# Solving a 64-token chunk by its 32x32 diagonal inverses instead of a 64x64 inverse, and a new order of small products in a TensorE-filled loop

## The chip, the cores and the metric

The kernel runs on one core of a Trainium2 chip. The time is device microseconds of one execution; the kernel before was run three times. All work of the program lies in one launch, and nothing is computed outside it.

## What is computed

The reference is one transformer block over x of shape (4, 2048, 256): a delta-rule linear attention with 4 heads of 64, in chunks of 64 tokens, and a gated MLP of four layers, each behind a layernorm whose scale, shift and gate come from a conditioning vector. Cut to what the change touches, for each sequence, head and chunk:

```python
A0 = -where(strict, (wk @ wk.T) * L, 0)        # 64 x 64, strictly lower
A = inv(eye - A0)                              # unit lower triangular
def step(S, ...):                              # over the 32 chunks
    v_new = A @ v - (A @ wk) @ S               # = A @ (v - wk @ S)
    o = rk_g @ S + intra @ v_new
    S = gamma_C * S + wk_g.T @ v_new
```

After it come the output product with Wr, the gated residual (x1), a second layernorm, and the MLP: `silu(h w1) * (h w2)` of width 1024, then two 1024 x 1024 layers with gelu (l2 and l3 below), then 1024 to 256 (y).

## The kernel before

The kernel walks 32 steps (`STEPS`), one for each chunk of 64 tokens of all 4 sequences, 256 tokens in all. The recurrence over the state S forces the order of the attention parts; the MLP has no such order. So the program is a pipeline written out by hand: in step n the PE stream is the l3 layer and the last product y of chunk n-2, then l1 and l2 of chunk n-1, and between these long, dense products stand short *visits* of the attention of chunk n. The steps 3 to 30 run in a loop whose body holds 14 of them (`PASS`), the others are written out. Step 0 runs alone (list `alone`), step 1 in two pieces (`opening`, `second`).

What stands where is told by the table `between` (lines 278 to 297 of the profile's file): its key is an MLP item such as ("l2", 1), the second of the eight output blocks of layer l2, and its value lists the parts that come behind it. `walk` runs through that order for **each engine in turn**, and every engine carries out its own share of each part (`part` in each engine's block); semaphores tie them together, and each engine works strictly in that order. The normalisation of the next chunk hangs on the same items (`next_norm`).

The MLP products are 128x128 weights times 256 columns in a single-pass format (w_hi with act_hi and act_lo). The attention works in fp32, where the trace has two MATMUL records for one product; a record is called a **pass** below. Its products are small and go to pieces of the array: `half(c)` names 64 partitions, the 64 tokens of the chunk for two of the four sequences; `quarter(c, i)` names 32 of them, i the first or second half of the chunk. (e, q) run over these two sequences times four heads, m = e * 4 + q from 0 to 7. The visits of the attention in a step, by PE lines:

- start: h and r are turned (L1087, L1091) into `duo[0]`, behind l2's last block
- long visit behind ("l3", 1): gram (L1109, into `duo[1]`), pred (L1115, into `duo[0]`), values (L1101, into `solo[0]`), inter (L1124)
- ("ln2", 0) behind ("l3", 5): the normalised x1, `xn2`, is turned (L1207, into `solo[1]`)
- n 1 to n 3 behind l1's blocks 1, 4 and 7: the 32x32 diagonal inverses by a series (L1143; L1145 and L1152; L1147), each with 32 or 64 products of 32x32
- mi behind ("l2", 1), L1161: 16 products of 32x32, corner of the matrix times the lower inverse; ACT copies the result to `mi` (L656)
- upd behind ("l2", 2), L1170: 16 more of 32x32, times the upper inverse; meanwhile ACT spreads `inv_t` into the block-diagonal 64x64 `invT` (L661), then copies the corner in (L668)
- new behind ("l2", 4), L1181: 16 products of 64x64, `invT` times the corrected values v, into `solo[1]`; ACT copies them to `vn` (L673)
- state behind ("l2", 5) (L1189, L1191) and attn_out behind ("l2", 6) (L1198)

On the other engines the parts that matter are: ACT copies of gram (L647), v (L643), o_state (L650); POOL multiplies gram by masks (L535, `lv`) and decays the state (L578); DVE makes `intra` (L806), subtracts the prediction from v (L813, `u_ready`), runs the substitution fs 0 to fs 3 (L817 on) on the first masked gram, and makes `xn2` (L875, part norm2). MLP work on ACT is L705 and L706, on DVE L776.

At the start of step 2 PE runs eight products into `solo[1]` that nothing reads (L1080) and then waits until the last weight blocks have been rounded on ACT and POOL (`rounded`).

## Time and profile before

| | us |
|---|---|
| three runs | 1855.87, 1856.35, 1859.41 |
| median | 1856.35 |
| profiled execution, its time | 1858.39 |
| its span | 1856.6 |
| PE busy | 1807.0 (97%) |
| DVE, ACT, POOL busy | 1147.4, 989.2, 613.3 |
| mean granted TensorE clock | 0.987 |

Read it by the spacing of the MATMUL records on PE: their durations overlap, so the distance from start to start is what a product costs. The profile's page shows a clock of 7 tenths in the first two of its 40 slices and 9 tenths or more in all others.

### The profile page before, as it was taken

What the parts mean: (1) busy time and instruction counts of PE and PEld (TensorE: products, weight loads), DVE (VectorE), ACT (ScalarE), POOL (GpSimd) and SP (SyncE); (2) the same over time, 40 slices, a digit from 0 to 9 for tenths busy, and PEclk for the clock granted to TensorE, in tenths of its full rate; (3) what the DMA queues carried; (4) which work ended last, traced back from release to release, by engine and by line L of the source; (5) the groups of instructions that cost most, each with busy time, mean ns of one, the idle gap of its engine ahead of it and who ended that gap; (6) DMA issues with size and microseconds to landing.
All of it is one profiled execution on the core that took longest, in us unless ns stands there. A gap on an engine that the chain in (4) does not pass through costs nothing.

```text
span 1856.6 us, 66857 instructions
## 1 busy us (share of the span) xinstructions
PE 1807.0 (97%) x28606; PEld 1725.4 (93%) x28606; DVE 1147.4 (62%) x3044; ACT 989.2 (53%) x2318; POOL 613.3 (33%) x691
## 2 busy tenths in 40 slices
PE   4699999999999999999999999999999999999998
PEld 3599999999999999999999999999999999999998
DVE  5665666665666665666665666665666665666632
ACT  5564555554555554555555555555555555555454
POOL 3343233333233333233333233233233333233211
PEclk7799999999999999999999999999999999999999
DMA  8000000000000000000000000000000000000000
GB/s 322 20 14 20 8 20 19 20 14 20 8 20 19 20 14 20 8 19 19 19 14 19 8 19 19 19 14 20 8 19 20 19 14 20 8 19 20 15 2 13
DMA packets 33011, 44.04 MB, mean 24 GB/s; under 512 B 8324, under 2 KB 24840, under 8 KB 32712
## 3 DMA queue, kind: packets, MB, share of 16 engines
q1 hardware_dynamic: 30736, 37.19, 6.7%
q8 instruction: 230, 3.77, 0.8%
q10 hardware_dynamic: 1976, 2.51, 0.5%
q14 instruction: 69, 0.57, 0.1%
HBM read 22.78 MB, written 8.39 MB: 17 GB/s over the span
## 4 chain that ended last, share of the span: by engine, by line
PE 94%; issue 2%; DVE 2%; POOL 1%; ACT 1%; ACTq 0%; POOLq 0%; DVEq 0%
PE mlp L991 61%; PE mlp L1050 6%; PE solo L991 4%; PE solo L1101 3%; PE duo L1198 3%; PE solo L1181 2%; PE duo L1147 1%; PE duo L1143 1%; PE duo L1145 1%; PE duo L1189 1%; PE duo L1161 1%; PE duo L1170 1%; PE duo L1152 1%; PE duo L1124 1%; PE duo L1109 1%
## 5 line engine op out<-in xcount | busy, mean ns | idle before, releaser
L991 PE MATMUL mlp<-act_hi,w_hi 128*128 128x256 f32 x4096 | 1005.5, 288 | 0.4 <-POOL act_lo L569 0.2
L991 PE MATMUL mlp<-act_lo,w_hi 128*128 128x256 f32 x4096 | 973.0, 279 | 0.0
L991 PEld LDWEIGHTS mlp<-act_hi,w_hi 128*128 128x128 f32 x4096 | 770.4, 188 | 13.4 <-POOL act_lo L569 0.4
L991 PEld LDWEIGHTS mlp<-act_lo,w_hi 128*128 128x128 f32 x4096 | 769.4, 188 | 0.8
L705 ACT ACTIVATE full<-mlp,scale_sb 128x256 f32<-128x256 f32 x512 | 244.2, 477 | 558.6 <-PE mlp L991 557.1
L776 DVE TENSOR_TENSOR act_lo<-full,act_hi 128x256 fp32r<-128x256 f32 x512 | 243.1, 475 | 415.6 <-ACT act_hi L706 415.6
L569 POOL TENSOR_TENSOR act_lo<-full,act_hi 128x256 fp32r<-128x256 f32 x256 | 186.9, 736 | 505.3 <-ACT act_hi L695 505.2
L706 ACT ACTIVATE act_hi<-mlp,scale_sb 128x256 fp32r<-128x256 f32 x512 | 240.7, 470 | 0.0
L991 PE MATMUL mlp<-xh,w_hi 128*128 128x256 f32 x768 | 182.7, 279 | 5.4 <-ACT w_hi L627 5.4
L535 POOL TENSOR_TENSOR lv<-gram,level_mask 128x256 f32<-128x256 f32 x192 | 158.0, 849 | 84.1 <-DVE low L817 79.7
L991 PE MATMUL mlp<-xl,w_hi 128*128 128x256 f32 x768 | 182.3, 279 | 0.0
L515 POOL TENSOR_TENSOR rstd<-ve,minus_half 128x2 f32<-128x2 f32 x64 | 49.4, 772 | 398.2 <-DVE ve L743 398.2
L991 PEld LDWEIGHTS mlp<-xh,w_hi 128*128 128x128 f32 x768 | 145.4, 189 | 5.6 <-ACT w_hi L627 5.6
L690 ACT ACTIVATE gate<-mlp,scale_sb 128x256 f32<-128x256 f32 x192 | 91.2, 475 | 111.1 <-PE mlp L991 100.0
L889 DVE SCALAR_TENSOR_TENSOR full<-mlp,scale_sb,gate 128x256 f32<-128x256 f32 x192 | 92.7, 483 | 88.1 <-ACT gate L690 88.0
L991 PEld LDWEIGHTS mlp<-xl,w_hi 128*128 128x128 f32 x768 | 145.5, 190 | 0.0
L1050 PE MATMUL mlp<-w_hi,act_hi 128*128 128x256 f32 x512 | 124.3, 284 | 0.7 <-DVE act_lo L776 0.6
L1050 PE MATMUL mlp<-w_hi,act_lo 128*128 128x256 f32 x512 | 124.0, 281 | 0.0
L515 POOL TENSOR_TENSOR rinv<-ssm,minus_half 128x8 f32<-128x8 f32 x32 | 52.5, 1642 | 203.0 <-DVE ssm L766 203.0
L695 ACT CAST act_hi<-full 128x256 fp32r<-128x256 f32 x256 | 101.8, 398 | 8.3 <-DVE full L889 8.3
L1050 PEld LDWEIGHTS mlp<-w_hi,act_hi 128*128 128x128 f32 x512 | 96.5, 188 | 1.1 <-DVE act_lo L776 1.1
L1050 PEld LDWEIGHTS mlp<-w_hi,act_lo 128*128 128x128 f32 x512 | 96.4, 188 | 0.0
(161 smaller groups left out, 2591.1 us busy)
## 6 DMA issues: line engine op xcount, KB each, us to landing
w_raw<-in_wts SPq DMA_DIRECT2D x22, 512.0 KB, 10.0
xin<-in_x SPq DMA_DIRECT2D x64, 128.0 KB
out_y<-y SPq DMA_DIRECT2D x64, 128.0 KB, 2.5
kg<-r SPq DMA_DIRECT2D x64, 126.0 KB
wmod_sb<-in_wmod ACTq DMA_DIRECT2D x1, 1024.0 KB, 8.1
kg<-last SPq DMA_DIRECT2D x64, 2.0 KB
last<-r SPq DMA_DIRECT2D x64, 2.0 KB, 1.7
wmod_sb<-in_wmod ACTq DMA_DIRECT2D x1, 512.0 KB, 4.9
```

Source lines behind the costliest of these rows:

```text
L515: pool.tensor_tensor(dst[:], src[:], minus_half[:, 0:src.shape[1]], ALU.pow).then_inc(done, 1)
L535: return pool.tensor_tensor(lv[slot][:, e].rearrange("p (b q) n -> p b (q n)", b=NB), gram[:, e].rearrange("p (b q) n -> p b (q n)", b=NB) ...
L569: pool.tensor_tensor(act_lo[0][:, k, :], full[k % 3][:], act_hi[0][:, k, :].bitcast(F32), ALU.subtract).then_inc(l_ready[0], 1)
L690: act.activation(gate[k % 2][:], gated[k % 3][:, 0:TOK], ACT.Silu, scale=scale_sb[:, 0, k:k + 1]).then_inc(l_act[0], 1)
L695: act.copy(act_hi[0][:, j, :], full[j % 3][:]).then_inc(l1_hi, 1)
L705: act.activation(full[k % 2][:], mlp[k % 2][:, 0:TOK], ACT.Gelu, scale=s)
L706: act.activation(act_hi[layer % 2][:, k, :], mlp[k % 2][:, 0:TOK], ACT.Gelu, scale=s).then_inc(l_act[layer], 1)
L776: dve.tensor_tensor(act_lo[layer % 2][:, k, :], full[k % 2][:], act_hi[layer % 2][:, k, :].bitcast(F32), ALU.subtract).then_inc(l_ready[la ...
L889: dve.scalar_tensor_tensor(full[k % 3][:], up, s, gate[k % 2][:], ALU.mult, ALU.mult).then_inc(prod_ready, 1)
L991: mm = pe.matmul(dst, *general_ops, start=is_first and i == 0, stop=is_last and i == 1)
L1050: mm = pe.matmul(mlp[k][:, 0:D], *ops, start=j == 0 and i == 0, stop=j == HK - 1 and i == 1)
L1101: mm = pe.matmul(solo[0][:, b * D:(b + 1) * D], hT[:, kt, b, :], wv_sb[:, kt, :], start=kt == 0, stop=kt == KT - 1)
```

## The change

The 64x64 inverse is no longer built. Part solve 0, behind ("l2", 1), holds mi's 16 products and 32 new ones: each 32x32 diagonal inverse times its 32 rows of v, 64 columns, into `solo[1]` ("own"). ACT then copies mi with its sign turned and copies the finished first halves of the chunk to `vn`, in two instructions of 32 partitions. Part solve 1, behind ("l2", 3), adds the corner: 16 products of `mi` (32x32) and those first halves (64 columns) onto the second halves that still lie in `solo[1]`; then ACT copies all of `vn`. The parts mi, upd and new, the tile `invT`, its four ACT instructions and two constant columns go.

In the long visit the order becomes values, pred, gram, inter, and behind inter the turning of `xn2` (part turn), which was a visit of its own behind ("l3", 5). norm2, DVE's share that makes `xn2`, moves from behind ("l3", 1) to behind ("l3", 0); ACT's and DVE's order in the long visit follows the table. pred waits for rT_ready itself, as it now comes ahead of gram. In step 1's opening, turn is split off from ln2 in the same place. The eight unread products of step 2 go, and the wait behind them is spread over that step's l3 blocks and y. `alone`, `alone_norm` and `second` follow with the new parts.

```diff
     between = {
-        ("l3", 1): [("gram", 0), ("pred", 0), ("values", 0), ("inter", 0), ("norm2", 0), ("intra", 0), ("u", 0)],
+        ("l3", 0): [("norm2", 0)],
+        ("l3", 1): [("values", 0), ("pred", 0), ("gram", 0), ("inter", 0), ("turn", 0), ("intra", 0), ("u", 0)],
...
         ("l1", 7): [("n", 3)],
-        ("l2", 1): [("keys", 0), ("mi", 0)],
-        ("l2", 2): [("upd", 0)],
-        ("l2", 4): [("new", 0)],
+        ("l2", 1): [("keys", 0), ("solve", 0)],
+        ("l2", 3): [("solve", 1)],
...
-    next_norm = {("n", 3): "stats", ("mi", 0): "norm", ("upd", 0): "square", ("l2", 3): "length", ("l2", 5): "unit"}
+    next_norm = {("n", 3): "stats", ("solve", 0): "norm", ("l2", 2): "square", ("l2", 3): "length", ("l2", 5): "unit"}
...
                         act.copy(square_t[:].rearrange("p k n -> p (k n)"), duo[0][:, 1, 0:2 * NP * HB]).then_inc(square_ready, 1)
-                    if name == "mi":
+                    if name == "solve" and k == 0:
                         act.wait_ge(mi_full, now)
-                        act.copy(mi[:].rearrange("p k n -> p (k n)"), duo[0][:, 0, 0:2 * NP * HB]).then_inc(mi_ready, 1)
-                    if name == "upd":
-                        act.wait_ge(inv_t_ready[1], now)
-                        for i in range(2):
-                            ins = act.activation(invT[:].rearrange("p e q n -> p (e q) n")[:, :, HB * i:HB * (i + 1)], inv_t[:],
...
-                        ins.then_inc(diag_ready, 1)
-                        act.wait_ge(diag_ready, now)
-                        act.wait_ge(upd_full, now)
+                        act.activation(mi[:].rearrange("p k n -> p (k n)"), duo[0][:, 0, 0:2 * NP * HB], ACT.Copy, scale=-1.0).then_inc(mi_ready, 1)
+                        act.wait_ge(own_full, now)
                         for c in range(2):
-                            ins = act.activation(invT[quarter(c, 0)].rearrange("p e q n -> p (e q) n")[:, :, HB:C],
-                                                 of_head(duo[0][quarter(c, 0), 1, 0:2 * NP * HB]), ACT.Copy, scale=-1.0)
-                        ins.then_inc(invT_ready, 1)
-                    if name == "new":
+                            ins = act.copy(vn[quarter(c, 0)].rearrange("p q e n -> p (q e n)"), solo[1][quarter(c, 0), :])
+                        ins.then_inc(own_ready, 1)
+                    if name == "solve" and k == 1:
...
                             pe.wait_ge(rounded[0], 5 + k)
+                        if i == 2 and isinstance(n, int) and n == 2:
+                            if k < 5:
+                                pe.wait_ge(rounded[0], 13 + k)
+                            else:
+                                pe.wait_ge(rounded[1], k - 4)
...
                         pe.wait_ge(l_act[2], nth(m, HK - 2))
+                    if isinstance(n, int) and n == 2:
+                        pe.wait_ge(rounded[1], SLOTS - 17)
...
                     if name == "start":
-                        if isinstance(n, int) and n == 2:
-                            for j in range(8):
-                                pe.matmul(solo[1][:], w_hi[:, j, :], w_hi[:, 4 * j:4 * j + 4, :].rearrange("p b n -> p (b n)"), start=True, stop=True)
-                            pe.wait_ge(rounded[0], 17)
-                            pe.wait_ge(rounded[1], SLOTS - 17)
...
                         pe.wait_ge(hT_ready, now)
+                        pe.wait_ge(rT_ready, now)
...
                             mm.then_inc(first_full, 1)
-                    if name == "mi":
+                    if name == "solve" and k == 0:
...
                         pe.wait_ge(inv_t_ready[1], now)
-                        for e, q, c, i in quarters:
-                            if i == 1:
-                                mm = pe.matmul(of_head(duo[0][quarter(c, 0), 0, 0:2 * NP * HB])[:, e * NP + q, :], lv[0][quarter(c, 1), e, q, 0:HB],
-                                               inv_t[quarter(c, 1), e * NP + q, :], start=True, stop=True)
-                        mm.then_inc(mi_full, 1)
-                    if name == "upd":
+                        pe.wait_ge(u_ready, now)
+                        for e in range(2):
+                            for q, (b, hp) in enumerate(pair_of):
+                                m, hd = e * NP + q, 2 * hp + e
+                                for c in range(2):
+                                    inner = pe.matmul(of_head(duo[0][quarter(c, 0), 0, 0:2 * NP * HB])[:, m, :], lv[0][quarter(c, 1), e, q, 0:HB],
+                                                      inv_t[quarter(c, 1), m, :], start=True, stop=True)
+                                for c, i in ((0, 0), (1, 0), (0, 1), (1, 1)):
+                                    rows = quarter(c, i)
+                                    mm = pe.matmul(solo[1][rows, q * P + DH * e:q * P + DH * e + DH], inv_t[rows, m, :],
+                                                   v[rows, b, hd * DH:(hd + 1) * DH], start=m == 0, stop=i == 0 and m == 2 * NP - 1)
+                        inner.then_inc(mi_full, 1)
+                        mm.then_inc(own_full, 1)
+                    if name == "solve" and k == 1:
...
                         pe.wait_ge(mi_ready, now)
+                        pe.wait_ge(own_ready, now)
                         for e, q, c, i in quarters:
-                            rows = quarter(c, i)
                             if i == 0:
-                                mm = pe.matmul(of_head(duo[0][rows, 1, 0:2 * NP * HB])[:, e * NP + q, :], inv[rows, e * NP + q, :],
-                                               mi[rows, e * NP + q, :], start=True, stop=True)
-                        mm.then_inc(upd_full, 1)
-                    if name == "new":
-                        pe.wait_ge(const_in, 16)
-                        pe.wait_ge(invT_ready, now)
-                        pe.wait_ge(u_ready, now)
-                        for q, (b, hp) in enumerate(pair_of):
-                            for e in range(2):
-                                hd = hp * 2 + e
-                                for c in range(2):
-                                    mm = pe.matmul(solo[1][half(c), q * P + DH * e:q * P + DH * e + DH], invT[half(c), e, q, :],
-                                                   v[half(c), b, hd * DH:(hd + 1) * DH], start=True, stop=True)
+                                mm = pe.matmul(solo[1][quarter(c, 1), q * P + DH * e:q * P + DH * e + DH], mi[quarter(c, 0), e * NP + q, :],
+                                               vn[quarter(c, 0), q, e, :], start=False, stop=e == 1 and q == NP - 1)
...
                         mm.then_inc(ao_full, 1)
-                    if name == "ln2" and k == 0:
+                    if name == "turn":
...
```

On PE, the long visit in the steady part before. Behind a name in brackets are the semaphores that the instruction waits for; a row counts products, not passes:

```order
L991 MATMUL mlp<-act_lo,w_hi 128x256
L1109 MATMUL duo<-rT 64x65 [waits rT_ready,const_in]
L1109 MATMUL duo<-rT 64x65 x15
L1115 MATMUL duo<-state,rT 64x64 [waits hT_ready,const_in]
L1115 MATMUL duo<-state,rT 64x64 x15
L1101 MATMUL solo<-wv_sb,hT 128x256 [waits prod_ready,hT_ready]
L1101 MATMUL solo<-wv_sb,hT 128x256 x3
L1124 MATMUL duo<-rg,state 64x64 [waits pred_full,rg_ready,const_in]
L1124 MATMUL duo<-rg,state 64x64 x15
L991 MATMUL mlp<-act_hi,w_hi 128x256 [waits l_act2]
```

And the same place of the changed kernel (its lines have other numbers: L1091 is values, L1106 pred, L1099 gram, L1115 inter, L1196 turn):

```order
L978 MATMUL mlp<-act_lo,w_hi 128x256
L1091 MATMUL solo<-wv_sb,hT 128x256 [waits prod_ready,hT_ready]
L1091 MATMUL solo<-wv_sb,hT 128x256 x3
L1106 MATMUL duo<-state,rT 64x64 [waits rT_ready,hT_ready,const_in]
L1106 MATMUL duo<-state,rT 64x64 x15
L1099 MATMUL duo<-rT 64x65 [waits rT_ready,const_in]
L1099 MATMUL duo<-rT 64x65 x15
L1115 MATMUL duo<-rg,state 64x64 [waits pred_full,rg_ready,const_in]
L1115 MATMUL duo<-rg,state 64x64 x15
L1196 MATMUL solo<-con,xn 128x128 [waits xn2_ready]
L1196 MATMUL solo<-con,xn 128x128 x3
L978 MATMUL mlp<-act_hi,w_hi 128x256 [waits l_act2]
```

The full-array products now stand at both ends, the 64x64 ones in one block between them, and the turning of `xn2` has joined the visit.

On ACT, from l2's second block to its fourth, before:

```order
L705 ACTIVATE full<-mlp,scale_sb 128x256 [waits l_ready0,l_full1]
L706 ACTIVATE act_hi<-mlp,scale_sb 128x256
L656 COPY mi<-duo 128x256 [waits mi_full]
L705 ACTIVATE full<-mlp,scale_sb 128x256 [waits l_ready1,l_full1]
L706 ACTIVATE act_hi<-mlp,scale_sb 128x256
L661 ACTIVATE invT<-inv_t,con 128x8x32 [waits inv_t_ready1]
L661 ACTIVATE invT<-inv_t,con 128x8x32
L668 ACTIVATE invT<-duo 32x8x32 [waits upd_full,diag_ready]
L668 ACTIVATE invT<-duo 32x8x32
L705 ACTIVATE full<-mlp,scale_sb 128x256 [waits l_ready1,l_full1]
L706 ACTIVATE act_hi<-mlp,scale_sb 128x256
```

And of the changed kernel, from the same block:

```order
L692 ACTIVATE full<-mlp,scale_sb 128x256 [waits l_ready0,l_full1]
L693 ACTIVATE act_hi<-mlp,scale_sb 128x256
L652 ACTIVATE mi<-duo 128x256 [waits mi_full]
L656 COPY vn<-solo 32x512 [waits own_full]
L656 COPY vn<-solo 32x512
L692 ACTIVATE full<-mlp,scale_sb 128x256 [waits l_ready1,l_full1]
L693 ACTIVATE act_hi<-mlp,scale_sb 128x256
L692 ACTIVATE full<-mlp,scale_sb 128x256 [waits l_ready1,l_full1]
L693 ACTIVATE act_hi<-mlp,scale_sb 128x256
L660 COPY vn<-solo 128x512 [waits vn_full]
```

The four instructions on `invT` are gone, two copies stand behind mi, and the copy of all of `vn` comes one block of l2 earlier.

PE's solve 0 in the changed kernel, the first rows of it, of which the last two repeat to the end of the part:

```order
L978 MATMUL mlp<-act_lo,w_hi 128x256
L1155 MATMUL duo<-inv_t,lv 32x32 [waits inv_t_ready1,u_ready,far_ready,const_in]
L1155 MATMUL duo<-inv_t,lv 32x32
L1159 MATMUL solo<-v,inv_t 32x64 x4
L1155 MATMUL duo<-inv_t,lv 32x32 x2
L1159 MATMUL solo<-v,inv_t 32x64 x4
```

Two corner products (L1155) and four diagonal ones (L1159) alternate, once for each of the 8 values of m; before, L1161 stood here alone with 16 products.

## Rows read from the trace of the kernel before

**Rows 1.** The page: span, busy time of each engine, and the chain's shares by engine.
```profile
span 1856.6 us, 66857 instructions
...
PE 1807.0 (97%) x28606; PEld 1725.4 (93%) x28606; DVE 1147.4 (62%) x3044; ACT 989.2 (53%) x2318; POOL 613.3 (33%) x691
...
PE 94%; issue 2%; DVE 2%; POOL 1%; ACT 1%; ACTq 0%; POOLq 0%; DVEq 0%
```

**Rows 2.** Timeline, PE, a long visit: start us, length us, line, passes.
```profile
900.89 0.28 PE L991 MATMUL mlp<-act_lo,w_hi 128*128 128x256 f32 x1
901.10 0.70 PE L1109 MATMUL duo<-rT 64*64 64x65 f32 x32
901.62 0.65 PE L1115 MATMUL duo<-state,rT 64*64 64x64 f32 x32
902.20 1.99 PE L1101 MATMUL solo<-wv_sb,hT 128*128 128x256 f32 x8
904.12 0.69 PE L1124 MATMUL duo<-rg,state 64*64 64x64 f32 x32
...
904.97 0.28 PE L991 MATMUL mlp<-act_lo,w_hi 128*128 128x256 f32 x1
```

**Rows 3.** Timeline, PE, the turning of xn2 in its own visit.
```profile
911.03 0.28 PE L991 MATMUL mlp<-act_lo,w_hi 128*128 128x256 f32 x1
...
912.20 0.28 PE L991 MATMUL mlp<-act_lo,w_hi 128*128 128x256 f32 x1
...
912.88 0.28 PE L991 MATMUL mlp<-act_lo,w_hi 128*128 128x256 f32 x1
```

**Rows 4.** Timeline, PE, around n 1 (64 passes) and n 2 (128 passes).
```profile
866.05 0.28 PE L991 MATMUL mlp<-xl,w_hi 128*128 128x256 f32 x1
...
867.16 0.28 PE L991 MATMUL solo<-xl,w_hi 128*128 128x256 f32 x1
...
869.67 0.28 PE L991 MATMUL mlp<-xl,w_hi 128*128 128x256 f32 x1
...
871.35 0.28 PE L991 MATMUL solo<-xl,w_hi 128*128 128x256 f32 x1
```

**Rows 5.** Timeline, PE, around mi and around new (32 passes each).
```profile
935.48 0.28 PE L991 MATMUL mlp<-act_lo,w_hi 128*128 128x256 f32 x1
...
936.53 0.28 PE L991 MATMUL mlp<-act_lo,w_hi 128*128 128x256 f32 x1
...
942.74 0.28 PE L991 MATMUL mlp<-act_lo,w_hi 128*128 128x256 f32 x1
...
944.25 0.28 PE L991 MATMUL mlp<-act_lo,w_hi 128*128 128x256 f32 x1
```

**Rows 6.** Timeline, ACT, from mi's copy to vn's.
```profile
936.52 0.38 ACT L656 COPY mi<-duo 128x256 f32<-128x256 f32 x1
938.50 0.47 ACT L705 ACTIVATE full<-mlp,scale_sb 128x256 f32<-128x256 f32 x1 [1.60 <-PE mlp L991]
...
944.14 0.59 ACT L673 COPY vn<-solo 128x512 f32<-128x512 f32 x1 [0.25 <-PE solo L1181]
```

**Rows 7.** Timeline, POOL, behind the gram of the long visit.
```profile
902.39 3.31 POOL L535 TENSOR_TENSOR lv<-gram,level_mask 128x256 f32<-128x256 f32 x4
```

**Rows 8.** Timeline, DVE, the same place.
```profile
908.13 1.13 DVE L817 TENSOR_REDUCE low<-lv 128x64 f32<-128x512 f32 x1
```

**Rows 9.** Timeline, PE, start of step 2.
```profile
114.36 2.01 PE L1080 MATMUL solo<-w_hi 128*128 128x512 f32 x8
116.38 0.66 PE L1087 MATMUL duo<-con,h 128*128 128x128 f32 x4
```

**Rows 10.** Timeline, PE, step 0, from mi to state.
```profile
50.67 1.06 PE L1161 MATMUL duo<-inv_t,lv 32*32 32x32 f32 x32 [1.10 <-DVE inv_t L852]
...
57.05 1.13 PE L1189 MATMUL duo<-intra,vn 64*64 64x64 f32 x32 [0.77 <-ACT vn L673]
```

**Rows 11.** Timeline, DVE, norm2 of step 32, which has no long visit.
```profile
1795.73 0.88 DVE L875 SCALAR_TENSOR_TENSOR xn<-x,mv,rstd 128x256 f32<-128x256 f32 x2
```

More of the change, by code:

```diff
@@ L66 @@
 CO_ROW = CO_TURN + P
-CO_BLK = CO_ROW + P
-CO_N = CO_BLK + 2
+CO_N = CO_ROW + P
 CHECKS = {0: (0,), 1: (1, 2, 3, 4, 5), 2: (6,), 3: (7, 8, 9, 10)}
@@ L94, in constants @@
     c[C - 1, CO_ROW:CO_ROW + P] = 1.0
-    for k in range(2):
-        c[:, CO_BLK + k] = j[:, 0] // HB == k
     c[:, CO_E] = np.e
@@ L219, in main @@
     inv_t = sb("inv_t", [2 * NP, HB])
-    invT = sb("invT", [2, NP, C])
     mi = sb("mi", [2 * NP, HB])
@@ L256, in main @@
     low_ready, sub_ready, term_ready = sem("low_ready"), sems("sub_ready", FS), sems("term_ready", FS - 1)
-    inv_ready, inv_t_ready, invT_ready = sems("inv_ready", 2), sems("inv_t_ready", 2), sem("invT_ready")
+    inv_ready, inv_t_ready = sems("inv_ready", 2), sems("inv_t_ready", 2)
     step_full, step_ready, step_t_ready, square_full, square_ready = (sem(k) for k in (
@@ L260, in main @@
     first_full, first_ready, rest_full = sem("first_full"), sem("first_ready"), sem("rest_full")
-    mi_full, mi_ready, upd_full, diag_ready = sem("mi_full"), sem("mi_ready"), sem("upd_full"), sem("diag_ready")
+    mi_full, mi_ready, own_full, own_ready = sem("mi_full"), sem("mi_ready"), sem("own_full"), sem("own_ready")
     pred_full, inter_full, u_ready, vn_full, vn_ready, ds_full, state_ready = (sem(k) for k in (
@@ L301, in main @@
         mixed += [item] + between.get(item, [])
-    next_norm = {("n", 3): "stats", ("mi", 0): "norm", ("upd", 0): "square", ("l2", 3): "length", ("l2", 5): "unit"}
+    next_norm = {("n", 3): "stats", ("solve", 0): "norm", ("l2", 2): "square", ("l2", 3): "length", ("l2", 5): "unit"}
     alone = [("check", 0), ("ready", 0), ("start", 0), ("spread", 0), ("tables", 0), ("gram", 0), ("pred", 0), ("values", 0), ("inter", 0), ("gates", 0), ("intra", 0),
              ("u", 0), ("fs", 0), ("fs", 1), ("fs", 2), ("fs", 3), ("expand", 0), ("far", 0), ("check", 1), ("round", 0), ("residual", 0), ("n", 1), ("n", 2),
-             ("check", 2), ("wr", 0), ("n", 3), ("keys", 0), ("mi", 0), ("upd", 0), ("new", 0), ("check", 3), ("state", 0), ("attn_out", 0)]
+             ("check", 2), ("wr", 0), ("n", 3), ("keys", 0), ("solve", 0), ("solve", 1), ("check", 3), ("state", 0), ("attn_out", 0)]
     def low_halves(words):
         return words.bitcast(U16).rearrange("p (n two) -> p two n", two=2)[:, 0, :]
-    alone_norm = {("n", 3): "stats", ("mi", 0): "norm", ("upd", 0): "square", ("new", 0): "length", ("state", 0): "unit"}
-    opening = [("start", 0), ("gram", 0), ("norm2", 0), ("ln2", 0), ("ln2", 1), ("pred", 0), ("values", 0), ("inter", 0), ("intra", 0), ("fs", 0), ("parts", 0),
+    alone_norm = {("n", 3): "stats", ("keys", 0): "norm", ("solve", 0): "square", ("solve", 1): "length", ("state", 0): "unit"}
+    opening = [("start", 0), ("gram", 0), ("norm2", 0), ("turn", 0), ("ln2", 0), ("ln2", 1), ("pred", 0), ("values", 0), ("inter", 0), ("intra", 0), ("fs", 0), ("parts", 0),
                ("round", 1), ("silu", 0)]
@@ L332, in walk @@
                     part(name, k)
-            elif name in ("l1", "l2", "l3", "norm2", "ln2", "parts", "silu"):
+            elif name in ("l1", "l2", "l3", "norm2", "turn", "ln2", "parts", "silu"):
                 if has_mlp:
```

1 line of the change is left out of this document (removed).

## The prediction, on record before the changed kernel ran

> **What bounds the kernel now.** First the page [rows 1]: PE is busy for 1807.0 us of a span of 1856.6 us and holds 94% of the chain that ended last, the other engines 4% together. So one microsecond of PE's stream is one microsecond of time, and work on ACT, DVE or POOL counts only where PE waits for it. Second, PE's timeline, by start-to-start distance. Ten passes of the MLP take 1.17 us [rows 3], 0.117 us each. A visit's cost is then the distance from the last MLP pass ahead of it to the second one behind it, less two of these, 0.234. That gives 3.84 us for the long visit (904.97 - 900.89 - 0.234) [rows 2], 0.446 for the turning of xn2 [rows 3], 0.876 for n 1 and 1.446 for n 2 [rows 4], 0.816 for mi and 1.276 for new [rows 5]. upd has mi's shape and cost, 0.82. In all 31 steps that have the last three, each repeats these within 0.01.
>
> **What a visit is made of.** n 1 and n 2 differ only in 64 more passes of 32x32, on the same four pieces of the array: 0.570 / 64 = 8.9 ns a pass. What is left of n 1 is 0.876 - 64 x 0.0089 = 0.31 us for going from full-array products to small ones and back. mi's 32 passes then take (0.816 - 0.31) / 32 = 15.8 ns: they use two pieces alternately, so one piece takes a pass every 32 ns. new's 64x64 passes take (1.276 - 0.31) / 32 = 30 ns, also on two pieces, 60 ns on one.
>
> **The long visit.** Before, it goes full, small (gram, pred), full (values), small (inter), full: two round trips. After, values comes first, straight behind the MLP, and pred, gram and inter stand together: one trip. That takes 0.31 away by the difference above; the trace shows no such row directly, so the bounds are 0.1 (the extra on re-entry alone) and 0.4, and I take 0.31 since the two trips and the passes add up to the visit's 3.84 (96 small passes at 15 ns, as new's two-piece pace halved over four pieces, are 1.45; 8 values passes at 1.92 / 8 = 0.24 less a share of the switches, about 1.75; 0.62 for the trips). turn keeps its 4 passes and 0.446: the array is back in full mode behind inter anyway. Over steps 2 to 31 this is 30 x 0.31 = 9.3 us.
>
> Waits there. turn needs norm2, which now starts behind l3's first block; it stands 3.5 us into the visit, and DVE has the 1.87 us of l3's second block besides, against 1.8 us of work. inter waits for pred to be complete; its cover shrinks from values' 1.92 us to gram's 0.52 (901.10 to 901.62) [rows 2], while a pass is 0.2 us long: still covered. gram's result comes about 2.3 us later, so POOL's masks start near T + 3.7 instead of T + 1.5 (T = 900.89) [rows 7] and the first two of the four are done near T + 5.4; DVE reads them at T + 7.2 [rows 8]. 1.8 us of slack remain, so this costs nothing. v's correction on DVE waits for o_state, which moves by less than 0.2.
>
> **The solve.** Removed: 0.82 + 0.82 + 1.28 = 2.92 us a step. Added, solve 1: 32 passes on two pieces, 32x32 weights, 64 columns. The trace has no such pass. From mi's (32 weights columns, 32 moving) to new's (64, 64) a piece's pass grows from 32 to 60 ns; this one grows one of the two, so I take the middle, 46 ns a piece and 23 a pass: 0.31 + 32 x 0.023 = 1.05. Bounds: mi's 0.82 and new's 1.28. Added, solve 0: 64 passes of the same kind on four pieces (16 on each, 16 x 0.046 = 0.74) and mi's 32 on two others (16 on each, 0.51), interleaved. All six pieces are different. If they run beside each other the longest piece, 0.74, or PE's issue decides; 96 passes at n 1's 8.9 ns are 0.85. With the trip 1.16; I take 1.20, as pieces share rows and columns. Bounds: n 1's 0.88, and 0.31 + 0.51 + 16 x 0.060 = 1.78 for mi first and then passes as slow as new's. Gain: 2.92 - 1.20 - 1.05 = 0.67 a step, 20.8 us over the 31 steps 1 to 31.
>
> Waits: solve 1 waits for ACT's copy of mi and the two of own, of at most 0.59 each (vn's length) [rows 6]. They start near 0.9 us into solve 0 and are done about 1.5 us later; solve 1 stands behind two blocks of l2, 3.74 us. Behind the copies on ACT are the next block's gelus, which before started 1.60 us after mi's copy had ended [rows 6]; two copies, 1.18, fit in that. DVE's and POOL's queues keep their order there, and SP issues the same transfers.
>
> **Once each.** The eight unread products go: 116.38 - 114.36 = 2.0 us [rows 9]; the waits behind them are due long before the blocks that now carry them, except that ACT and POOL finish rounding about 2 us into the step, and l3's first block needs an earlier slot. Step 0 takes 6.38 us from mi to state [rows 10] at half clock, with three hand-overs to ACT; two hand-overs and fewer visits make it about 5.5: 0.9. Step 32 has no long visit to cover norm2 (0.88 us) [rows 11], so turn waits: a loss of 0.3, between 0 and 1.
>
> **Sum.** 9.3 + 20.8 + 2.0 + 0.9 - 0.3 = 32.7 us. The profiled execution took 1858.39; 1825.7 for such a one. The median of the runs is 2.0 lower: 1856.35 - 32.7 = 1823.7, said as **1824 us**.
>
> **Rivals.** A: pieces in the same rows do not run beside each other. Then in solve 0 the second row quarter holds own's 16 passes and mi's 16: 0.31 + 16 x (0.046 + 0.032) = 1.56, the gain falls by 0.36 x 31 = 11 us: **1835 us**. For it: in mi and n each row quarter is used by one piece only. Against it: gram and new send passes to row halves in the same alternation, but gram, which changes the columns too, takes 0.52 / 32 = 16 ns a pass [rows 2] and new 30. A row half shared by two pieces thus did twice the work. The Trainium skill, "TensorE: Matmul & The Clock Gate", Part 3, states this rival as a rule: a weight load overlaps products in flight only where the row group differs. By that the sum is the 1835; gram's row speaks against it.
>
> B, slower: the interleaving of two kinds of pass, or adding onto what lies in PSUM, stops the overlap, and every pass goes at new's 30 ns. solve 0 is then 0.31 + 96 x 0.030 = 3.19 and solve 1 1.28, together 1.55 over the 2.92: 48 us lost, 12 gained elsewhere, **1892 us**. It decides from the point where solve 0 exceeds 2.25 us, 20 ns a pass. Against it: n 1 has 64 passes in 0.57. The same page, Part 1, gives a floor of about 25 ns from start to start however small the product; by that solve 0 would be an estimated 2.7 us and the kernel 1872, but n 1's 8.9 ns [rows 4] contradicts it.
>
> C: a hand-over becomes late every step (own's copies to solve 1, gram's to the substitution) by about 1 us: 31 us, and the time is **1855**, no change. It needs slacks of 1.8 to 2.2 us to be used up first.
>
> D: the interleaving is free and the switches cost more than taken: solve 0 1.0, solve 1 0.9, trip 0.4: 1810.
>
> **Chances.** Forecast 0.64 (1815 to 1832), A 0.19, D 0.09, C 0.03, B 0.05. The range 1810 to 1842 takes in the forecast and A with a part of C's smaller form, and leaves out some of D. A measurement of this kernel tells about 0.2%, 3.7 us, from no change. Faster by more: 0.92; within: 0.03; slower: 0.05.
>
> **What would show it.** In PE's timeline behind l3's second block: a visit of about 3.98 us with turn inside (3.84 - 0.31 + 0.446). Behind l2's second block one of 1.20, behind the fourth one of 1.05, nothing behind the third and fifth; 1.56 at the first would be A, over 2.25 B. Steps 0.98 us shorter, with no idle PE ahead of pred, inter, turn or solve 1; the list of waits should still have no PE entry of more than a few times. DVE's L817 successor should start at the same distance behind the visit. The forecast is wrong if PE shows a recurring wait for ACT, or if its issue stalls, now a few single ones, come in every step with the added passes.

## The result: 1842 us, less than half of the gain that was forecast

| | before | changed |
|---|---|---|
| median of the runs (4 each) | 1856.11 | 1842.28 |
| lowest and highest | 1853.27, 1859.41 | 1841.56, 1844.15 |
| span of the profiled execution | 1856.6 | 1840.8 |
| PE busy | 1807.0 | 1784.0 |

The ratio of the medians is 0.9926, with a 95% interval of 0.9908 to 0.9945: faster by 13.8 us, where 1824.0 was forecast and the range ended at 1842. The page of the changed kernel, its span, busy times and the shares of the chain by engine, which answer to [rows 1]:

```profile
span 1840.8 us, 68798 instructions
...
PE 1784.0 (97%) x29622; PEld 1706.7 (93%) x29622; DVE 1149.1 (62%) x3044; ACT 972.2 (53%) x2254; POOL 602.2 (33%) x691
...
PE 78%; DVE 15%; issue 4%; ACT 1%; POOL 1%; ACTq 0%; DVEq 0%; POOLq 0%
```

PE lost 23 us of busy time, where the forecast's two large terms were 30. But PE's share of the chain that ended last fell from 94% to 78%, and DVE's rose from 2% to 15%: in every step the chain now leaves PE and runs through DVE for a stretch.

**Where it leaves.** The list of waits names the place. Its columns are the waiting engine and line, what released it, total us, times, longest. The first row is of the changed kernel, and PEld is the weight load of y's products, which take `act_lo` as their weights:

```profile
PEld mlp L1045 <- DVE act_lo L763: 11.9, 31, 1.3
```

In the kernel before, the same group of weight loads (there L1050) idled for 1.1 us in all:

```profile
L1050 PEld LDWEIGHTS mlp<-w_hi,act_hi 128*128 128x128 f32 x512 | 96.5, 188 | 1.1 <-DVE act_lo L776 1.1
```

On PE's timeline of the changed kernel, y's passes stand 0.12 us apart but at one place, in every step, 0.41 and then 0.22. That is the first pass that needs the eighth block of l3:

```profile
907.87 0.28 PE L1045 MATMUL mlp<-w_hi,act_hi 128*128 128x256 f32 x1
907.99 0.28 PE L1045 MATMUL mlp<-w_hi,act_lo 128*128 128x256 f32 x1
908.40 0.38 PE L1045 MATMUL mlp<-w_hi,act_hi 128*128 128x256 f32 x1
908.62 0.28 PE L1045 MATMUL mlp<-w_hi,act_lo 128*128 128x256 f32 x1
```

0.41 + 0.22 - 2 x 0.117 is 0.40 us a step. Summed over all steps from the starts, y loses 15.5 us; before, 2.8. Not all of the 15.5 is waiting: in step 31 y waits twice for DVE, and behind the second wait its passes go 0.21 us apart instead of 0.12:

```profile
1738.04 0.39 PE L1045 MATMUL mlp<-w_hi,act_hi 128*128 128x256 f32 x1 [1.08 <-DVE act_lo L763]
1739.16 0.39 PE L1045 MATMUL mlp<-w_hi,act_hi 128*128 128x256 f32 x1 [0.62 <-DVE act_lo L763]
```

From 1739.4 to 1742.8 us the granted clock was 0.50, the lower of its two levels. That costs 16 passes 1.5 us, so the waits are 14.0. In the kernel before y waits at the same two places of step 31 (it loses 1.3 us there), and the clock stays up.

**The stretch of DVE behind it.** DVE in the changed kernel, from v's correction, just ahead of its last wait for ACT, to the piece of l3's last block. A number in brackets is the idle time before the instruction and who ended it:

```profile
895.78 0.68 DVE L800 TENSOR_TENSOR v<-v,duo 128x512 f32<-128x512 f32 x1
898.19 0.78 DVE L763 TENSOR_TENSOR act_lo<-full,act_hi 128x256 fp32r<-128x256 f32 x1 [1.74 <-ACT act_hi L693]
898.90 1.20 DVE L804 TENSOR_REDUCE low<-lv 128x64 f32<-128x512 f32 x1
...
900.88 0.41 DVE L763 TENSOR_TENSOR act_lo<-full,act_hi 128x256 fp32r<-128x256 f32 x1
...
907.60 0.45 DVE L826 STREAM_TRANSPOSE inv_t<-inv 128x256 f32<-128x256 f32 x1
907.96 0.38 DVE L763 TENSOR_TENSOR act_lo<-full,act_hi 128x256 fp32r<-128x256 f32 x1
```

From 898.19 to 908.34 no row has an idle time: the reduction `low`, the four fs parts, the expansion and six pieces `act_lo` go without a break, and the last `act_lo` is what y waits for. Ahead of this stretch DVE idles for 1.74 us. In the kernel before, the last `act_lo` of the stretch had a gap before it, 0.42 us spent waiting for ACT:

```profile
916.75 0.45 DVE L839 STREAM_TRANSPOSE inv_t<-inv 128x256 f32<-128x256 f32 x1
917.62 0.42 DVE L776 TENSOR_TENSOR act_lo<-full,act_hi 128x256 fp32r<-128x256 f32 x1 [0.42 <-ACT act_hi L706]
```

Two things used that gap up and went past it. The 0.446 us visit of turn behind l3's sixth block no longer delays PE inside this stretch, so PE reaches y that much earlier. And `act_lo` of l3's third block takes 0.78 us where it took 0.43 (at 907.79 before). POOL's rows of the changed kernel tell why:

```profile
894.87 2.82 POOL L531 TENSOR_TENSOR lv<-gram,level_mask 128x256 f32<-128x256 f32 x4 [2.11 <-ACT gram L643]
897.65 1.04 POOL L574 TENSOR_TENSOR state<-state,chunk_decay 128x512 f32<-128x512 f32 x1
```

POOL is ready for the masks 2.11 us before ACT's copy of gram lets them start, so the decay of the state behind them now lies at 897.65 to 898.69, beside this `act_lo`. Before, it ran from 905.67 to 906.70, beside v's correction and an idle DVE. An estimate from these rows: the visit's 0.446 and the 0.35 that `act_lo` grew, less the gap of 0.42, make 0.38 us a step; y loses 0.34 a step more than before.

**The visits.** PE's long visit of the changed kernel, which answers to [rows 2]:

```profile
891.26 0.28 PE L978 MATMUL mlp<-act_lo,w_hi 128*128 128x256 f32 x1
891.38 1.89 PE L1091 MATMUL solo<-wv_sb,hT 128*128 128x256 f32 x8
893.20 0.69 PE L1106 MATMUL duo<-state,rT 64*64 64x64 f32 x32
893.71 0.65 PE L1099 MATMUL duo<-rT 64*64 64x65 f32 x32
894.18 0.65 PE L1115 MATMUL duo<-rg,state 64*64 64x64 f32 x32
894.75 0.66 PE L1196 MATMUL solo<-con,xn 128*128 128x128 f32 x4
...
895.37 0.28 PE L978 MATMUL mlp<-act_lo,w_hi 128*128 128x256 f32 x1
```

895.37 - 891.26 - 0.234 = 3.88 us with turn inside, against 3.84 + 0.446 = 4.29 before. The two visits of the solve, PE passes around them, which answer to [rows 5]:

```profile
925.70 0.27 PE L978 MATMUL mlp<-act_lo,w_hi 128*128 128x256 f32 x1
...
927.21 0.28 PE L978 MATMUL mlp<-act_lo,w_hi 128*128 128x256 f32 x1
...
930.72 0.27 PE L978 MATMUL mlp<-act_lo,w_hi 128*128 128x256 f32 x1
...
932.16 0.28 PE L978 MATMUL mlp<-act_lo,w_hi 128*128 128x256 f32 x1
```

By the same rule solve 0 costs 1.28 and solve 1 1.21; the medians over the 31 steps are 1.29 and 1.21, so 2.50 in place of 2.92.

**The ledger of the two spans**, all from starts on PE, summed over all steps:

| from before to changed | us |
|---|---|
| long visit and turn, steps 2 to 31 | -12.0 |
| turn alone in step 32 (0.45 to 0.98) | +0.5 |
| solve, 31 steps | -13.0 |
| start of step 2 (2.97 to 0.89) | -2.1 |
| other visits, among them n 2's single stalls in issue (+3.8) and one of 1.5 less at a start | +2.1 |
| waits inside y | +11.2 |
| half clock inside y of step 31 | +1.5 |
| full clock 3.2 us later, at half pace | +1.6 |
| pace of the MLP's passes, 116.9 to 116.5 ns, some 11,200 of them | -4.9 |
| not assigned | -0.7 |
| sum | -15.8 |

The pace is not shown to be the change's doing: over eight profiled executions, each of another kernel, it lies between 116.5 and 117.0 ns, and the kernel with 117.0 (e2 below) has the same solve as the one with 116.5. Whether it differs from kernel to kernel or from execution to execution was not tried. So spans of single executions tell 5 us apart at best, and the verdicts below go by the runs, with the mechanism read from the places in the trace.

### The profile page after: what moved, and what is told of

Read it like the earlier page. It is cut to its first block, busy times and chain, and to the rows that moved or that the text cites. A ratio compares the mean times of both kernels' runs of the same rounds, so it can differ in the third digit from the quotient of the medians.

```text
span 1840.8 us, 68798 instructions
## 1 busy us (share of the span) xinstructions
PE 1784.0 (97%) x29622; PEld 1706.7 (93%) x29622; DVE 1149.1 (62%) x3044; ACT 972.2 (53%) x2254; POOL 602.2 (33%) x691
## 4 chain that ended last, share of the span: by engine, by line
PE 78%; DVE 15%; issue 4%; ACT 1%; POOL 1%; ACTq 0%; DVEq 0%; POOLq 0%
PE mlp L978 48%; PE mlp L1045 4%; PE solo L978 4%; PE duo L1187 3%; PE solo L1091 3%; DVE sub_term L817 3%; DVE act_lo L763 3%; DVE sub_row L815 2%; DVE sub L819 2%; PE solo L1170 2%; DVE low L804 2%; PE solo L1159 1%; PE duo L1134 1%; PE duo L1138 1%; PE duo L1136 1%
## 5 line engine op out<-in xcount | busy, mean ns | idle before, releaser
L978 PE MATMUL mlp<-act_hi,w_hi 128*128 128x256 f32 x4096 | 994.1, 285 | 0.3 <-POOL act_lo L565 0.2
L763 DVE TENSOR_TENSOR act_lo<-full,act_hi 128x256 fp32r<-128x256 f32 x512 | 249.1, 487 | 373.9 <-ACT act_hi L693 371.9
L531 POOL TENSOR_TENSOR lv<-gram,level_mask 128x256 f32<-128x256 f32 x192 | 143.9, 777 | 107.6 <-ACT gram L643 62.8
L1045 PE MATMUL mlp<-w_hi,act_hi 128*128 128x256 f32 x512 | 128.4, 289 | 5.6 <-DVE act_lo L763 1.9
```

The costliest lines, as they stand in the source:

```text
L531: return pool.tensor_tensor(lv[slot][:, e].rearrange("p (b q) n -> p b (q n)", b=NB), gram[:, e].rearrange("p (b q) n -> p b (q n)", b=NB) ...
L763: dve.tensor_tensor(act_lo[layer % 2][:, k, :], full[k % 2][:], act_hi[layer % 2][:, k, :].bitcast(F32), ALU.subtract).then_inc(l_ready[la ...
L978: mm = pe.matmul(dst, *general_ops, start=is_first and i == 0, stop=is_last and i == 1)
L1045: mm = pe.matmul(mlp[k][:, 0:D], *ops, start=j == 0 and i == 0, stop=j == HK - 1 and i == 1)
```

## Experiments

The theory that these rows suggest, S: in l3 DVE's stretch has become the bound, so y waits 0.4 us a step. Its rivals were that the wait comes from the solve's new copies, from the long visit's own order, or from the 0.446 us visit that was taken out of the stretch.

**e1, fs 0 a block earlier.** The reduction `low` and the first fs part move from behind l3's third block to the end of the list behind its second, into DVE's idle 1.74 us:

```diff
-        ("l3", 1): [("values", 0), ("pred", 0), ("gram", 0), ("inter", 0), ("turn", 0), ("intra", 0), ("u", 0)],
-        ("l3", 2): [("fs", 0)],
+        ("l3", 1): [("values", 0), ("pred", 0), ("gram", 0), ("inter", 0), ("turn", 0), ("intra", 0), ("u", 0), ("fs", 0)],
+        ("l3", 2): [],
```

> The changed kernel with one edit: DVE's first substitution part, fs 0, stands behind u in the long visit instead of behind l3's third block, so DVE does it in the 1.7 us in which it now waits for that block. Theory S (the y product waits for DVE's last act_lo, because DVE has been busy without a gap since l3's third block): the wait inside y, 0.40 us a step, falls to at most 0.06, as before the change; 31 steps give 11 us, about 1831 us against 1842. Rival R (the wait is ACT's, whose gelus and layernorm copies of l3's last blocks are no earlier, or PE's own): the wait stays and the time stays at 1842 within 2 us.

Measured: 1833.67 us (1831.07 to 1837.37), ratio to before 0.9869 (0.985 to 0.9887), where the changed kernel has 0.9926. The last `act_lo` waits for ACT again:

```profile
907.69 0.45 DVE L826 STREAM_TRANSPOSE inv_t<-inv 128x256 f32<-128x256 f32 x1
908.73 0.43 DVE L763 TENSOR_TENSOR act_lo<-full,act_hi 128x256 fp32r<-128x256 f32 x1 [0.59 <-ACT act_hi L693]
```

What y loses falls from 15.5 to 3.3 us in all; the two long waits of step 31 are gone too. The time, 1833.67, is somewhat above the 1831 expected. DVE and POOL still meet: `act_lo` of l3's third block now takes 1.02 us (from 899.77), beside a mask of POOL. No product was removed and no engine made faster; the same DVE work was put where DVE had been idle. S stands.

**e2, turn back in its old place.** This separates the two causes within S: the lost 0.446 us visit (S1), and POOL's decay beside `act_lo` (S2).

```diff
-        ("l3", 1): [("values", 0), ("pred", 0), ("gram", 0), ("inter", 0), ("turn", 0), ("intra", 0), ("u", 0)],
+        ("l3", 1): [("values", 0), ("pred", 0), ("gram", 0), ("inter", 0), ("intra", 0), ("u", 0)],
...
-        ("l3", 5): [("ln2", 0), ("fs", 3)],
+        ("l3", 5): [("turn", 0), ("ln2", 0), ("fs", 3)],
```

> The changed kernel with turn back in a visit of its own behind l3's sixth block, ahead of ln2; values first and norm2 early stay. Theory S1 (turn's 0.446 us had been cover for DVE's chain in l3, moving it ahead took this from the chain's time): long visit 3.44, turn 0.45, the sum as now, and the wait inside y falls by 0.35 to about 0.05, 1831 us. Rival S2 (the later gram is what made DVE late: POOL's masks and state decay now run beside DVE's act_lo and substitution and stretch them): at least half of the wait stays, 1836 to 1842 us.

Measured: 1844.54 us (1841.85 to 1846.68), ratio 0.9923 (0.9907 to 0.994); y still loses 10.8 us. The long visit costs 3.48 and turn 0.44, together 3.93, so joining turn is itself worth 0.05. In this kernel `act_lo` of l3's third block took 1.19 us beside the decay: the visit's cover came back, and the overlap on POOL took it away again. In the steady steps 0.24 of the 0.34 us are left. S1 alone fell. The time is above even S2's 1836 to 1842, and the runs don't show the 4 us that y lost less than in the changed kernel: the MLP's pace in this profiled execution was the slowest of all, which is worth about 6 us. Why is open.

**e3 and e4, each half alone.** e3 is the kernel before with the new long visit and the split of turn; e4 is the changed kernel with the old long visit and turn in its old place. The core of e3's edit, of which e4's is the reverse:

```diff
-        ("l3", 1): [("gram", 0), ("pred", 0), ("values", 0), ("inter", 0), ("norm2", 0), ("intra", 0), ("u", 0)],
+        ("l3", 0): [("norm2", 0)],
+        ("l3", 1): [("values", 0), ("pred", 0), ("gram", 0), ("inter", 0), ("turn", 0), ("intra", 0), ("u", 0)],
```

> The kernel before with the long visit's part of the change alone (values first, norm2 early, turn at its end), mi, upd, new and the eight unread products as before. Theory S: long visit 3.88 where 3.84 and 0.446 stood, 0.405 less in 30 steps, 12.2 us, and 0.35 more wait inside y in 31, 10.9 us; together -1 us, about 1855 us, not to be told from before. Rival R (the wait inside y belongs to the solve's part): no wait, about 1844 us.

> The changed kernel with the long visit undone (gram, pred, values, inter, norm2 in it, turn behind l3's sixth block), the solve in two visits and no unread products. Theory S: solve 0 1.28 and solve 1 1.21 against 2.92, 0.43 less in 31 steps, 13.3 us, and 2.0 us once, no wait inside y beyond 0.05: 1841 us, the same as the whole change. Rival R (the solve's part makes the wait inside y): the wait stays at 0.3 or more and the time is 1850 or above.

Measured: e3 1858.1 us, ratio 1.0007 (0.9996 to 1.0018), y's waits 14.7; e4 1840.78 us (1838.32 to 1842.25), ratio 0.9905 (0.9888 to 0.9921), y's waits 2.7. The weight loads of y in e3 and in e4, with their idle time last:

```profile
L1051 PEld LDWEIGHTS mlp<-w_hi,act_hi 128*128 128x128 f32 x512 | 96.5, 189 | 12.7 <-DVE act_lo L777 12.6
```

```profile
L1044 PEld LDWEIGHTS mlp<-w_hi,act_hi 128*128 128x128 f32 x512 | 96.7, 189 | 1.2 <-DVE act_lo L762 1.2
```

So the wait belongs to the long visit and not to the solve. The long visit's 12 us are real on PE (3.88 in e3 too), and y gives back about as much: alone it changes nothing that can be measured. e4, with the solve and without the eight unread products, has all of the changed kernel's gain.

**e5 and e6, the decay elsewhere.** POOL's decay of the state leaves the long visit for the place of solve 1, where it follows POOL's `rinv` and nothing waits for it closely; e6 has e1's edit as well.

```diff
-                    if name == "inter":
+                    if name == "solve" and k == 1:
```

> The changed kernel with one edit on POOL: the decay of the state stands behind solve 1 instead of behind the masks of the long visit, where DVE is idle. In the changed kernel it runs beside DVE's act_lo of l3's third block, which takes 0.78 us there and 0.43 before. Theory S2 (POOL beside DVE stretches DVE's chain, and that is the larger part of what made DVE late): act_lo back to 0.43, the wait inside y falls from 0.40 to about 0.1, 1833 us. Rival S1 (only the 0.446 us that turn no longer covers counts): the wait stays above 0.3, 1841 us.

> Both edits: fs 0 ahead of l3's third block (e1) and the state's decay behind solve 1 (e5). If the wait inside y was all that DVE's lateness cost, the second edit finds at most the 0.01 us a step that e1 left and the time is e1's, 1833 us within 1; if DVE's lateness also costs elsewhere, it is 1 to 3 us less.

Measured: e5 1835.47 us (1833.16 to 1836.41), ratio 0.9886 (0.9867 to 0.9905); e6 1830.93 us (1827.3 to 1832.44), ratio 0.9863 (0.9843 to 0.9882). In e5 the piece of l3's third block is back at its old length, and `low` starts 7.28 us behind the long visit's beginning (at 888.12 there) in place of 7.64:

```profile
895.05 0.42 DVE L763 TENSOR_TENSOR act_lo<-full,act_hi 128x256 fp32r<-128x256 f32 x1 [1.73 <-ACT act_hi L693]
895.40 1.18 DVE L804 TENSOR_REDUCE low<-lv 128x64 f32<-128x512 f32 x1
```

Beside 0.78 in the changed kernel this 0.42 is the contention by itself: the same instruction on the same data, with and without POOL's `TENSOR_TENSOR` next to it. y loses 4.8 us in e5 and 3.0 in e6. The estimate from above comes out: 0.446 - 0.42 is 0.03 us a step for e5, where 0.04 is measured. Either edit alone recovers most of what y lost; with both the median is the lowest, 27 us below before. None of the intervals of e1, e5 and e6 touches that of the changed kernel. But e6's overlaps both others', so that two edits beat one is not shown, and what e6 was to decide, whether DVE's lateness also costs outside y, stays open.

e6 does show that the long visit was worth making: its interval lies below that of e4 (0.9888 to 0.9921), which has the same solve and the old long visit, and the medians are 10 us apart. With DVE's stretch relieved, most of the visit's 12 us arrive.

**e7 and e8, the passes' own price.** e7 issues every corner product of solve 1 twice (32 more passes), e8 every product of a diagonal inverse with v in solve 0 (64 more); both change the values that the kernel computes, and each was run once.

```diff
-                        for e, q, c, i in quarters:
+                        for rep, (e, q, c, i) in [(r, t) for r in range(2) for t in quarters]:
...
-                                for c, i in ((0, 0), (1, 0), (0, 1), (1, 1)):
+                                for rep, c, i in [(r, c, i) for r in range(2) for i in range(2) for c in range(2)]:
```

> The changed kernel with solve 1's 16 products made twice, so that the corner's term is taken off twice and what is computed is another thing. It measures one pass: 32 more, on the same two pieces. Theory P1 (a pass of 32x32 weights and 64 columns takes 28 ns on two pieces, and the change of mode the 0.31 that was taken): the visit grows from 1.21 to 2.11 us. Rival P2 (the pass is the 23 ns of the prediction and going to these pieces and back costs 0.47): 1.95 us.

> The changed kernel with own's 32 products of solve 0 made twice, added up, so that the values come out doubled there and what is computed is another thing. 64 more passes on four pieces. Theory P1 (a piece takes 56 ns for such a pass): the visit grows by 16 x 0.056 = 0.90 us, from 1.29 to 2.2. Rival P3 (the pieces are not full in solve 0, PE's issue at about 10 ns a pass is the limit, (1.29 - 0.31) / 96): it grows by 0.65, to 1.94.

Measured from the visits, as the spans have the pace's 5 us in them. e7's solve 1, with its 64 passes:

```profile
949.13 0.28 PE L978 MATMUL mlp<-act_lo,w_hi 128*128 128x256 f32 x1
949.34 1.98 PE L1170 MATMUL solo<-vn,mi 32*32 32x64 f32 x64
...
951.47 0.28 PE L978 MATMUL mlp<-act_lo,w_hi 128*128 128x256 f32 x1
```

951.47 - 949.13 - 0.234 = 2.11 us, so 32 passes add 0.90: 28 ns a pass, 56 on a piece, which is P1's visit of 2.11. The 0.31 for the trip is what is left of the single visit: 1.21 - 0.90. In e8 solve 0 costs 2.13 in the steps without a stall, 0.84 more for 64 passes: 13.1 ns a pass, 52 on a piece. That is nearer to P1's 2.2 than to P3's 1.94. e8's time, 1884.2 us, is 42 above the changed kernel's: 26 are the visits, and PE's stalls in issue grew by some 9 (6.2 us at the doubled line, 3.5 behind it); of the rest, 1.5 us are a stretch at a granted clock of 0.50 behind such a stall (from 1401.7 to 1405.1 us), and some 5 are not assigned. e7's is 1875.43, 33 above, of which the visits are 28.

**e9, the corner's products first.** In solve 0 all 16 corner products come ahead of the 32 others instead of between them.

```diff
+                        for e in range(2):
+                            for q, (b, hp) in enumerate(pair_of):
+                                m, hd = e * NP + q, 2 * hp + e
                                 for c, i in ((0, 0), (1, 0), (0, 1), (1, 1)):
```

> The changed kernel with the two kinds of product of solve 0 no longer alternating: first the 16 corner products (32 passes, on two pieces of the array), then the 32 products of the diagonal inverses with v (64 passes, on four other pieces). The same products, waits and copies. Theory Q (pieces run beside each other, and alternating is what hides the corner's passes): the two blocks add up, 32 passes at the old mi's 15.8 ns and 64 at the 13.3 ns that issuing the diagonal products twice added: 0.31 + 0.51 + 0.85 = 1.67 us in place of 1.29, 0.38 x 31 = 11.8 us more, a span of about 1853. Rival R (PE only works through a list of passes at some 10 ns each, whatever piece they are on): the visit stays at 1.29 and the span at 1841. Rival P (pieces in the same rows don't run beside each other, in whatever order): alternating hid nothing, so the visit stays at 1.29 as well.

Measured: 1858.11 us in one run, and the visit costs 1.64 us in place of 1.29, in all 31 steps:

```profile
935.68 0.28 PE L978 MATMUL mlp<-act_lo,w_hi 128*128 128x256 f32 x1
935.88 0.60 PE L1154 MATMUL duo<-inv_t,lv 32*32 32x32 f32 x26
...
936.39 1.00 PE L1161 MATMUL solo<-v,inv_t 32*32 32x64 f32 x58
...
937.54 0.28 PE L978 MATMUL mlp<-act_lo,w_hi 128*128 128x256 f32 x1
```

Q is right, R and P are out. If pieces in the same rows kept each other waiting, a row group used by both kinds would need 16 x 0.052 + 16 x 0.032 = 1.34 us, and the alternating visit's 96 passes take 0.98. The corner's 0.51 us costs only 1.29 - 0.31 - 0.84 = 0.14 when alternating, though four of the six pieces share rows with another.

## Why the prediction was wrong

**The visits: right in kind, 5 us short in sum.** PE's own saving came out at 12.0 + 13.0 + 2.1 - 0.5 = 26.6 us of the 31.8 forecast for the same items.
- Long visit: the forecast was 3.98, it is 3.88. The trip was under-sized: 0.40 a step with turn's share, not 0.31. e2's trace separates 0.35 for the order from 0.05 for turn. The bounds, 0.1 and 0.4, held for the order.
- Solve 1: forecast 1.05, measured 1.21. The failed term is the 46 ns of a 64-column pass on a piece, "the middle" between mi's 32 and new's 60; e7 measures 56. Here the number of moving columns set the price (32 ns with 32 columns, 52 to 56 with 64, both with 32x32 weights), and the size of the weights hardly counted (60 ns with 64x64).
- Solve 0: forecast 1.20, measured 1.29. The forecast went by PE's issue, 96 passes at 8.9 ns or 0.85, as the longest piece was put at 16 x 0.046 = 0.74. By e8 the passes on a piece take 52 ns, 0.84 together, and the corner, not quite hidden, adds 0.14. The structure was right: e9 shows that pieces run beside each other. Rival A's 1.56 did not come, and neither did a pass as slow as B's 30 ns: 1.29 is (1.29 - 0.31) / 96 = 10 ns a pass. With them fell what the Trainium skill, "TensorE: Matmul & The Clock Gate", states in Part 3 (overlap only where the row group differs), as far as it bears on these small fp32 products, and the floor in its Part 1.
- Together the solve gave 0.42 a step, not 0.67, so 13.0 us instead of 20.8. That is 7.8 of the 18.9 us missing (32.7 less 13.8); the long visit gave 2.7 back, y took 12.7, of which 11.2 are waits and 1.5 the half clock in step 31.
- Filler: 2.1 measured for 2.0. None of the spread waits shows at step 2.
- Step 32: 0.98 for turn alone, a loss of 0.5, within "between 0 and 1".

**Waits: the step that failed.** The prediction had the hand-over in hand: gram's masks come later, DVE reads them with 1.8 us of slack, "so this costs nothing". The arithmetic was right; in the changed kernel `low` is not delayed by the masks. But slack was checked only at the *first reader*. Two further questions were not put. What else does POOL do behind the masks, and beside which DVE instruction does it now fall? (The decay, beside `act_lo`: 0.35 us.) And how much slack has the *end* of DVE's stretch, once a 0.446 us visit no longer holds PE back inside it? (0.42, the gap ahead of the last `act_lo`, for which the prediction had no row.) Of this visit the prediction told only what its 4 passes cost, which is PE's side; that it was also cover for DVE was missed. The first question had a rule to answer it. The Trainium skill, "SBUF — State Buffer", section "SBUF: two separate sides", states that a VectorE instruction with two inputs in SBUF and a GpSimd instruction that reads SBUF exclude each other, and that the one that starts first blocks the other. The trace agrees: the decay started first both times, and `act_lo` ended 0.28 us behind the decay's recorded end in the changed kernel (898.97 and 898.69) and in e2 as well, where the decay ran from 902.10 to 903.14 and `act_lo` ended at 903.42. It made no difference that it had started 0.50 us before that end in the one and 0.91 in the other. The kernel before had the same sign in every step: its `act_lo` at 902.08 takes 0.60 us and ends at 902.68, POOL's `rg` beside it at 902.40. Rival C named "a hand-over becomes late every step", but in the wrong places (own's copies, gram's masks) and with a slack of 1.8 to 2.2 us ahead of it, and so it had 0.03. What happened is C at 0.4 us a step. The prediction's own sign, a recurring wait of PE, did come, 31 times, but for DVE and not for ACT, where it told the reader to look.

**Step 0: nothing of the 0.9.** PE's rows of step 0 in the changed kernel, which answer to [rows 10]:

```profile
50.71 0.27 PE L1155 MATMUL duo<-inv_t,lv 32*32 32x32 f32 x2 [1.22 <-DVE inv_t L839]
...
54.37 1.92 PE L1170 MATMUL solo<-vn,mi 32*32 32x64 f32 x32 [1.46 <-ACT vn L656]
57.05 1.14 PE L1178 MATMUL duo<-intra,vn 64*64 64x64 f32 x32 [0.77 <-ACT vn L660]
```

state starts at 57.05 in both. One hand-over is gone, but solve 1 waits 1.46 us for ACT, whose two copies of 32 partitions take 1.15 us together. A copy of a quarter of the partitions costs as much as one of all of them (0.56 and 0.58 against 0.59): here the length followed the 512 elements of a row. Copies of 256 elements took 0.37 to 0.39, with 32 partitions (L668 before) and with 128 (L652).

**The clock.** In the changed kernel the granted clock rises at 87.4 us, before at 84.2, with the first MLP pass at 81.4 in both; the page shows it as PEclk 6 where it was 7 in the second slice. The granted clock is 0.50, the lower level, in the stretch from 84 to 86 us here, and 0.96 before; PE is busy all the time from 82 us in both. In the other kernels the distance from that first pass to the rise is 3.0 (e6), 3.2 (e3), 4.2 (e5), 4.4 (e4), 5.8 (e1) and 5.9 us (e2): it differs between kernels with the same solve, so it is not shown to be the change's doing. The fall in step 31, behind PE's two waits for DVE, comes in e9 as well and in e8, but not in e2, e3 and e7, whose y waits as long there. Neither was in the prediction; together they are worth 3 us of the profiled execution.

**Issue.** The forecast's last sentence feared stalls in every step. They don't come in every step, but n 2's are more: six of them for 6.4 us in the changed kernel, 3.6 before, 3.5 in e4, and 5.0 to 6.9 in all kernels with the new long visit. One of the six, 2.65 us in step 0, is in the kernel before too. What ties them to it was not tried.

## What to carry to other kernels

When PE's stream gets shorter, look for the last instruction of each helper engine's unbroken stretch and read the idle time in front of it: that gap, and not the slack of the first instruction that the change delays, is what the shortening may use. A short visit in a dense stream is cover for the engines behind it, so taking it away has a second price. If a stretch without idle time has appeared, first look ahead of it: here 1.74 us of idle DVE stood right before it, and moving one part there was worth 9 us (1842.28 to 1833.67), beside the 14 that the whole change had brought.

## What was not expected of the hardware

- VectorE and GpSimd slow each other: DVE's 128x256 `TENSOR_TENSOR` on two SBUF operands takes 0.42 us alone, 0.78 when 0.50 us of POOL's decay is still to run as it starts, and 1.19 with 0.91 us still to run. In the kernels before and changed, e2 and e3, from 100 us on, every `act_lo` of DVE that takes over 0.55 us ends 0.27 to 0.29 us behind the recorded end of the POOL instruction that was running when it started, mostly the decay, `rg` or the residual's `base`. The other way round, a mask of POOL takes 0.88 to 0.91 us beside DVE's `xn2` in the kernel before and 0.74 without it. The correction of v, which reads one operand from PSUM, takes 0.68 beside the masks and 0.69 beside the decay.
- Small products on different pieces of the array run beside each other even where the pieces share rows: 96 passes of 32x32 weights in 0.98 us when two kinds alternate, 1.33 when they stand in blocks. In these runs what counted was how many different pieces were in use at once.
- A pass with 64 moving columns holds its piece for 52 to 56 ns with 32x32 weights, and new's 64x64 for 60; one with 32 columns for 32.
- The pace of the MLP's passes at full clock differs by 0.4% from one profiled execution to another, each of another kernel.
